# A feed-forward bias taken from a TensorE product and given to VectorE, in a macaron block

## The reference, cut to what matters

```
x = x + 0.5 * ffn(layernorm(x))                 # x: 8 x 512 x 128, float32
x = x + attn(layernorm(x))                      # 16 heads
x = x + 0.5 * ffn(layernorm(x))                 # the same weights again

def ffn(x):                                     # 3 blocks
    h = x
    for blk in range(3):
        i0, i1 = 2 * blk, 2 * blk + 1
        y = qlora_linear(h, ..., biases[i0], ...)      # 128 -> 128
        y = layernorm(y) * ln_gamma[blk] + ln_beta[blk]
        y = gelu(y)
        y = qlora_linear(y, ..., biases[i1], ...)
        h = y + h
    return h
```

## Time and profile before

| | us |
|---|---|
| median of 3 runs | 1030.14 |
| lowest and highest run | 1028.14, 1032.29 |
| the profiled execution's own time | 1026.52 |
| its span, first to last instruction | 1024.7 |
| mean granted TensorE clock | 0.979 of full |

### The profile page before, as it was taken

One profiled execution on the slowest core, in us unless ns is written; L12 is line 12 of the kernel. 1 busy time (PEld: TensorE's weight loads), 2 busy tenths in 40 slices (PEclk: granted clock), 3 DMA queues, 4 the chain that ended last, 5 costly groups with the idle time before them and its releaser, 6 DMA issues.

```text
span 1024.7 us, 22051 instructions
## 1 busy us (share of the span) xinstructions
PE 963.4 (94%) x5892; PEld 502.3 (49%) x5892; DVE 877.1 (86%) x1786; ACT 802.6 (78%) x1293; POOL 784.4 (77%) x706
## 2 busy tenths in 40 slices
PE   4895689999999999999999999999999999997897
PEld 4763234444444444444444444444444444444775
DVE  7667898988888889898888888888888888898566
ACT  4885388888888888888888888888888888886874
POOL 2644168888888888888888888888888888886442
PEclk9999699999999999999999999999999999998999
DMA  9000222222222222222222222222222222220002
GB/s 244 1 2 0 51 50 55 62 61 62 63 63 64 64 65 63 64 64 63 63 64 65 63 64 61 61 61 61 61 61 61 61 61 61 61 62 1 1 1 83
DMA packets 71676, 59.03 MB, mean 58 GB/s; under 512 B 11168, under 2 KB 70560, under 8 KB 71648
## 3 DMA queue, kind: packets, MB, share of 16 engines
q1 hardware_dynamic: 71392, 58.31, 24.0%
q10 hardware_dynamic: 256, 0.39, 0.1%
HBM read 6.23 MB, written 2.10 MB: 8 GB/s over the span
## 4 chain that ended last, share of the span: by engine, by line
PE 83%; DVE 10%; ACT 3%; POOL 2%; issue 1%; DMA 1%; SPq 0%; DVEq 0%; POOLq 0%; ACTq 0%
PE ps L1032 11%; PE ps L1034 10%; PE ps L1033 10%; PE ps L1022 10%; PE ps L1023 10%; PE ps L1015 6%; PE ps L1007 3%; PE ps L953 3%; PE ps L1048 3%; PE ps L1044 3%; PE ps L1045 3%; PE ps L1009 3%; PE ps L1008 3%; PE ps L925 2%; DVE stats L654 1%
## 5 line engine op out<-in xcount | busy, mean ns | idle before, releaser
L376 POOL TENSOR_TENSOR p_lo<-work_b,p_hi 128x1024 f16<-128x1024 f32 x256 | 539.8, 2130 | 129.4 <-ACT p_hi L527 129.3
L794 DVE TENSOR_REDUCE mcol<-ps 128x2 f16<-128x1024 f32 x256 | 301.0, 1220 | 0.8 <-PE ps L1015 0.7
L522 ACT ACTIVATE work_b<-ps,exp_scale 128x1024 f32<-128x1024 f32 x256 | 271.6, 1111 | 32.4 <-PE ps L1023 32.3
L527 ACT ACTIVATE p_hi<-work_b 128x1024 f16<-128x1024 f32 x256 | 256.0, 1054 | 0.0
L1022 PE MATMUL ps<-head_ops 128*128 128x512 f16 x512 | 195.1, 381 | 4.1 <-DVE mcol L794 2.0
L1032 PE MATMUL ps<-p_hi,xn_hi 128*128 128x512 f16 x512 | 195.2, 381 | 0.0
L1023 PE MATMUL ps<-head_ops 128*128 128x512 f16 x512 | 195.1, 381 | 0.0
L1033 PE MATMUL ps<-p_hi,xn_lo 128*128 128x512 f16 x512 | 194.4, 380 | 0.0
L1034 PE MATMUL ps<-p_lo,xn_hi 128*128 128x512 f16 x512 | 194.3, 379 | 0.0
L382 POOL TENSOR_TENSOR x<-x,o_sb 128x512 f32 (+1 forms) x128 | 162.7, 1271 | 8.7 <-DVE o_sb L819 8.7
L804 DVE STREAM_TRANSPOSE head_ops<-mcol 32x128 f16<-32x128 f16 x512 | 155.5, 304 | 9.3
(11 more groups left out here) (116 smaller groups left out, 1316.9 us busy)
## 6 DMA issues: line engine op xcount, KB each, us to landing
head_ops<-pair_ops SPq DMA_DIRECT2D x512, 64.0 KB, 2.0
head_ops<-pair_ops SPq DMA_DIRECT2D x128, 128.0 KB, 2.4
x<-x_dram SPq DMA_DIRECT2D x8, 256.0 KB, 5.9
out<-x SPq DMA_DIRECT2D x8, 256.0 KB, 3.0
vo_last<-wvo_dram SPq DMA_DIRECT2D x1, 1024.0 KB, 13.5
qk<-wq_dram SPq DMA_DIRECT2D x1, 512.0 KB, 5.6
qk<-wk_dram SPq DMA_DIRECT2D x1, 512.0 KB, 6.4
scl<-scales_dram ACTq DMA_DIRECT2D x8, 48.0 KB, 5.2
```

The costliest lines, as they stand in the source:

```text
L376: pool.tensor_tensor(p_lo[:, par, rows, :], p32[:, par, rows, :], p_hi[:, par, rows, :], ALU.subtract).then_inc(plo_done, 1)
L522: nc.scalar.activation(p32[:, par, 2 * a:2 * a + 2, :], s_ps[a], ACT.Exp, scale=exp_scale[:, 0:1]).then_inc(exp_done, 1)
L527: nc.scalar.activation(p_hi[:, par, 2 * a:2 * a + 2, :], p32[:, par, 2 * a:2 * a + 2, :], ACT.Copy).then_inc(phi_done, 1)
L794: nc.vector.tensor_reduce(mcol[:, par, :, t, 0], s_ps[t % 2], AX.X, ALU.max, negate=True).then_inc(max_red, 1)
```

## The change

The bias product of `lin1` and everything that prepared it is gone. The kernel gets the biases once more, as rows in DRAM (`brow_d`); ScalarE's queue loads the three rows of the first linears, spread to all 128 partitions, into `bias_rows` (now float32). VectorE takes the mean of each row and subtracts it (five instructions). A new `add_bias(f, i)` on VectorE adds the row to `bank[b]` and writes `work_b`, once for each batch of a unit. `squares` then reads `work_b` and writes its squares (which nothing reads) to the bank, and `z_scaled` multiplies `work_b` in place. The additions of units 0 and 1 stand ahead of the norm's means (for f = 0 between and behind the statistics); those of units 2 and 3 stand in rounds 1 and 2 in front of the seed; those of units 4 to 11 at the end of rounds 3 to 10. `weight_maxima(0)` and `(1)` move to rounds 0 and 1, in front of `z_scaled`.

```diff
+            act.dma_start(bias_rows[:, :, :], brow_d[0:NL:2, :].partition_broadcast(128)).then_inc(bias_in, 16)
...
                 for c, b in unit_batches(i):
-                    act.wait_ge(lin1_done, at(f, i, c))
+                    act.wait_ge(zb_ready, at(f, i, c))
...
-                        ins = nc.scalar.activation(work_b[:, b, cols], bank[b][:, cols], ACT.Square,
+                        ins = nc.scalar.activation(bank[b][:, cols], work_b[:, b, cols], ACT.Square,
...
-            link(dve, nc.vector.tensor_tensor(bias_c[:, :], bias[:, 0:NL:2], ps[:, SG + 2, 0:NL:2], ALU.subtract))
-            link(dve, nc.vector.tensor_tensor(bias_mid[:, :], bias_c[:, :], bf16_top(bias_c), ALU.subtract))
-            nc.vector.tensor_copy(bias_parts[:, :, 0], bf16_top(bias_c))
-            nc.vector.tensor_copy(bias_parts[:, :, 1], bf16_top(bias_mid))
-            nc.vector.tensor_tensor(bias_parts[:, :, 2], bias_mid[:, :], bf16_top(bias_mid),
-                                    ALU.subtract).then_inc(bias_split, 1)
...
+            dve.wait_ge(bias_in, 16)
+            link(dve, nc.vector.tensor_reduce(row_mean[:, :], bias_rows[:, :, :], AX.X, ALU.add))
+            link(dve, nc.vector.tensor_scalar(row_mean[:, :], row_mean[:, :], -1.0 / D, None, ALU.mult))
+            for n in range(NB):
+                ins = nc.vector.tensor_scalar(bias_rows[:, n, :], bias_rows[:, n, :], row_mean[:, n:n + 1], None,
+                                              ALU.add)
+            link(dve, ins)
+
+            def add_bias(f, i):
+                n = i // UNITS
+                row = bias_rows[:, n, :].rearrange("p (a d) -> p a d", a=1).to_broadcast([128, TT, D])
+                for c, b in unit_batches(i):
+                    dve.wait_ge(lin1_done, at(f, i, c))
+                    nc.vector.tensor_tensor(work_b[:, b, :].rearrange("p (t d) -> p t d", d=D),
+                                            bank[b].rearrange("p (t d) -> p t d", d=D), row,
+                                            ALU.add).then_inc(zb_ready, 1)
...
-                    nc.vector.tensor_tensor(work_b[:, b, :].rearrange(tiles, d=D), bank[b].rearrange(tiles, d=D),
-                                            scale.to_broadcast([128, TT, D]), ALU.mult).then_inc(z_full, 1)
+                    zb = work_b[:, b, :].rearrange(tiles, d=D)
+                    nc.vector.tensor_tensor(zb, zb, scale.to_broadcast([128, TT, D]), ALU.mult).then_inc(z_full, 1)
...
                 if f:
+                    add_bias(f, 0)
                     norm_stats([B - 1])
+                    add_bias(f, 1)
                 else:
-                    norm_stats(range(SG, B), loaded=True)
+                    norm_stats(range(SG, SG + 2), loaded=True)
+                    add_bias(f, 0)
+                    norm_stats(range(SG + 2, B), loaded=True)
+                    add_bias(f, 1)
                 norm_means(1)
...
+                    if i in (1, 2):
+                        add_bias(f, i + 1)
                     if i < STEPS:
                         seed(f, i)
+                    if f == 0 and i in (0, 1):
+                        weight_maxima(i)
                     if 1 <= i <= STEPS:
                         z_scaled(f, i - 1)
-                    if f == 0 and i in (2, 3):
-                        weight_maxima(i - 2)
+                    if 3 <= i < STEPS - 1:
+                        add_bias(f, i + 1)
...
-                    nc.tensor.matmul(bank[b].rearrange("p (t d) -> p t d", d=D), ones_b[:, :], row,
-                                     start=True, stop=False)
                     for t in range(TT):
                         ins = nc.tensor.matmul(bank[b][:, t * D:(t + 1) * D], hT[:, b, t * 128:(t + 1) * 128],
-                                               wt[:, 2 * n, :], start=False, stop=(t == TT - 1))
+                                               wt[:, 2 * n, :], start=True, stop=True)
```

More of the change, by code:

```diff
@@ L19, with macaron @@
 AX = mybir.AxisListType
-def macaron(nc, x_d, q_d, k_d, vo_d, qw_d, sc_d, bias_d, la_d, lb_d, gam_d, bet_d, out_d):
+def macaron(nc, x_d, q_d, k_d, vo_d, qw_d, sc_d, bias_d, la_d, lb_d, gam_d, bet_d, brow_d, out_d):
     B, T, D = x_d.shape
@@ L56, in macaron @@
         ident = sb("ident", [128, 128])
-        ident_b = sb("ident_b", [128, 128], BF16)
         mean_mat = sb("mean_mat", [128, 128])
@@ L101, in macaron @@
         u_u = sb("u_u", [128, 2 * TT])
[L102 to L105, removed]
+        bias_rows = sb("bias_rows", [128, NB, D])
+        row_mean = sb("row_mean", [128, NB])
         hT = sb("hT", [128, B, T])
@@ L147, in macaron @@
         prep_pe = sem("prep_pe")
[L148 to L151, removed]
+        bias_in = sem("bias_in")
+        zb_ready = sem("zb_ready")
         prep_v = sem("prep_v")
@@ L311, in _ @@
             pool.memset(mean_mat[:, :], 1.0 / D).then_inc(consts, 1)
-            pool.memset(ones_b[:, :], 1.0)
-            pool.memset(bias_rows[:, :, :], 0.0).then_inc(bias_clear, 1)
             pool.wait_ge(prep_p, 1)
@@ L357, in _ @@
                     fold_last(4 * i + 2)
-            pool.wait_ge(prep_a, 3)
+            pool.wait_ge(prep_a, 2)
             pool.tensor_tensor(w_lo[:, :, :], qk32[:, :, :], w_hi[:, :, :], ALU.subtract).then_inc(prep_p, 1)
-            pool.wait_ge(prep_a, 5)
+            pool.wait_ge(prep_a, 4)
             pool.tensor_tensor(vo_lo[:, :, :], vo32[:, :, :], vo_hi[:, :, 0:D], ALU.subtract).then_inc(prep_p, 1)
@@ L416, in _ @@
                 act.dma_start(scl[16 * s:16 * s + 16, :, :], sc_d[s].partition_broadcast(16)).then_inc(sc_in, 16)
-            act.wait_ge(consts, 2)
-            nc.scalar.activation(ident_b[:, :], ident[:, :], ACT.Copy).then_inc(prep_a, 1)
+            act.dma_start(bias_rows[:, :, :], brow_d[0:NL:2, :].partition_broadcast(128)).then_inc(bias_in, 16)
             def pre(f, s):
@@ L462, in weight_halves @@
                 if i == 10:
-                    act.wait_ge(prep_a, 2)
+                    act.wait_ge(prep_a, 1)
                     for n in range(2):
@@ L486, in ffn @@
                 pre(f, 0)
[L487 to L491, removed]
                 for i in range(STEPS + 3):
@@ L886, in _ @@
             pe.wait_ge(consts, 2)
-            nc.tensor.matmul(ps[:, SG + 2, 0:NL], mean_mat[:, :], bias[:, :], start=True, stop=True)
             for n in range(NL):
@@ L904, in pre @@
                     turn(bank[b], lambda t: xhat[:, b * TT + t, :], pre_t)
-            def turn_bias():
-                pe.wait_ge(bias_split, 1)
-                pe.wait_ge(prep_a, 1)
-                for n in range(NB):
-                    ins = nc.tensor.matmul(ps[0:3, SG + 3, n * D:(n + 1) * D], bias_parts[:, n, :], ident_b[:, :],
-                                           start=True, stop=True)
-                ins.then_inc(bias_turned, 1)
             def lin1(f, i):
@@ L920, in lin1 @@
                         pe.wait_ge(h_ready, (f * NB + n - 1) * B + b + 1)
-                    row = bias_rows[:, n, :].rearrange("p (a d) -> p a d", a=1).to_broadcast([128, TT, D])
-                    nc.tensor.matmul(bank[b].rearrange("p (t d) -> p t d", d=D), ones_b[:, :], row,
-                                     start=True, stop=False)
                     for t in range(TT):
                         ins = nc.tensor.matmul(bank[b][:, t * D:(t + 1) * D], hT[:, b, t * 128:(t + 1) * 128],
-                                               wt[:, 2 * n, :], start=False, stop=(t == TT - 1))
+                                               wt[:, 2 * n, :], start=True, stop=True)
                     ins.then_inc(lin1_done, 1)
@@ L967, in ffn @@
                     pre(0, 0)
-                    turn_bias()
                     pe.wait_ge(prep_v, 1)
-                    pe.wait_ge(bias_ready, 1)
                 for i in range(STEPS + 3):
@@ L995, in _ @@
             ffn(0)
-            pe.wait_ge(prep_a, 5)
+            pe.wait_ge(prep_a, 4)
             pe.wait_ge(prep_p, 10)
@@ L1148 @@
         "ln_beta": a["L0_ffn_ln_beta"].T,
+        "bias_rows": a["L0_ffn_biases"],
     }
```

3 lines of the change are left out of this document (removed).

## The result

| | before | after |
|---|---|---|
| median of 4 runs each, us | 1029.14 | 1053.95 |
| lowest to highest, us | 1027.93 to 1032.29 | 1053.64 to 1054.76 |
| profiled execution, us | 1026.52 | 1053.9 |
| its span, us | 1024.7 | 1052.0 |

The ratio is 1.0232 with an interval of 1.0206 to 1.0258: the change costs 24.8 us. The prediction had the direction (+12.9 us) and half the size, and 1053.95 lies outside its range of 1035 to 1051.

The account below looks back on a forecast made before the run. TensorE was taken to bound the steady steps, with VectorE's and GpSimd's queues holding the heads. Second feed-forward +2.8, first +6.6, operand places +2, clock +1.5: +12.9 on 1030.14, so 1043.0 us, range 1035 to 1051.

Parts of the forecast that it names:

- Read and write places: Both feed-forwards: z with two SBUF operands and GpSimd's Newton pieces hold each other up; +2 us, bounds 0 to +7.
- port: The prediction's word for z with two SBUF operands and GpSimd's Newton holding each other up; +2 us taken.
- Squares from SBUF into PSUM: ScalarE's squares, eight per step: ±0.03 us each, so ±2 us in the second feed-forward, ±1 in the first; taken as nothing.
- First feed-forward, head: Start of the first feed-forward: work added on VectorE delays seeds and z; +5.9 us where TensorE resumes, +6.6 to its end.
- Second feed-forward, head: Start of the second feed-forward: additions before the norm delay transposes 2.6 us and unit 4's product about 3.4 us.
- faster rival: Additions ahead of the norm fall into VectorE's waits, heads cost nothing, TensorE's savings remain: −4.7, 1025 us; chance 0.04.
- what stands in front of the norm is paid in full: Heads of both feed-forwards: work put on VectorE before the norm delays the chain by its full length; four additions, 2.6 us.
- The steady step: Second feed-forward's steady steps: VectorE and ScalarE in turn set 4.54 us, not 4.81; −1.9 us over seven steps.
- TensorE would show as no longer full: Sign in the profile after: steady steps near 4.55 to 4.7 us, TensorE no longer full, VectorE above 90%.
- TensorE's clock: TensorE's clock falls at a new place; +1.5 us, bounds 0 and 2.
- Hidden: ScalarE's new load and the removed bias preparation cost or gain nothing; without cover, each below 0.5 us.

Follow-up runs that it names:

- e1: Changed kernel, with GpSimd's two long subtractions started only after z of unit 11 of the first feed-forward; 1047.33 us, ratio 1.0172.
- e2: Changed kernel, with the bias added in place in PSUM, where squares and z read it; 1039.24 us, ratio 1.0104 to the kernel before.
- e9: Changed kernel, with the squares' unused output written to SBUF instead of PSUM, still reading SBUF; 1051.94 us, ratio 1.0217.
- e12: Changed kernel with the sum left in PSUM and no additions for units 0 to 3 (that computation left out); 1030.62 us, ratio 0.9995.
- e10: Changed kernel, with additions of units 0 and 1 behind the second half's norm and ScalarE's order fitted to it; 1054.52 us, ratio 1.0240.
- e8: Changed kernel, with 30 unused transposes on TensorE before its wait for weight_maxima(2) in the first feed-forward; 1049.76 us, ratio 1.0181.
- e7: Kernel before, with additions in place in PSUM for units 4 to 11 of the second feed-forward, seed between the two z; 1028.03 us, ratio 0.9974.
- e6: Kernel before, with additions in place in PSUM replacing the bias product for units 4 to 11 of the second feed-forward only; 1027.29 us, ratio 0.9960.

## Why the prediction was right in direction and short in size

**The account.** Of the 24.8 us, 6.6 are z 11 beside the long subtractions (after minus e1). 8.1 are the rest of what e2 gained (e1 minus e2): some 6 for the operands' places, and some 2 for TensorE's lower clock in the head, which is in the profiles of after and e1 and not in those of e2 and e9. 9.7 are left in e2, and the additions of the first four units account for all of them (e12). Together 24.4.

**The step that failed: "Read and write places".** It had the right instructions and the right mechanism, and was mis-sized: +2, with bounds of 0 and +7, where e2 shows 14.7 together with the squares, or some 12.7 without the head's clock. Two things were left out. The bound was built from z against Newton's pieces of 0.2 us; but GpSimd's queue also holds two subtractions of 4 us, and the trace of before had both facts (`w_lo` from 85.82 to 89.90, z 11 at 87.46 in 1.28 us). Each z of unit 11 waited for the end of the subtraction that was running, so the longest neighbour sets the bound, and 6.6 us lay there. Secondly, in the GpSimd-paced head each z holds up a Newton (a piece of 0.65 us at 51.57, 0.20 otherwise) and is itself held up by a fold (2.33 us for the pair at 49.83), and the z come one after another on the chain: 2.6 us from z 1 to z 4 (after against e2). The rows at 101.01 to 110.01 show the waiting, 7.90 us against e1's 1.28. What in the chip makes the two wait, for which the prediction has the name port, no run shows.

**"Squares from SBUF into PSUM" taken as nothing.** That was the second miss. The eight pairs take 2.46 us instead of 2.19, 0.03 each (0.27 over eight, 34 ns), the size and sign that the earlier trace rows had shown for a read; they were rounded away. Over seven steps it is 1.9 us, about two thirds of the 2.9 by which e2's second feed-forward beats after's (71.8 against 74.7); three of the squares on the first's chain add 0.8. The place of the result made no difference: the eight pairs take 2.46 us with either destination (after, e9).

**"First feed-forward, head" and "Second feed-forward, head": right in mechanism, and the close sum is in part luck.** Seed 0 was put at 32.1 and came at 32.33. With operands in PSUM, TensorE resumed 6.8 us later (e2), where 5.9 was predicted. e2's whole of +9.7 stands against 9.4 for the two feed-forwards and 1.5 for the clock, but the parts are not as predicted. In e2's profile the first feed-forward is 9.9 us longer than in that of before (6.6 predicted; the terms given for it add to 6.4), the second 1.1 (2.8 predicted), and the attention 1.6. Of the 9.9, 2.9 are two `lin2` at a lower clock: 3.18 us instead of 1.72 behind the gap (0.66 over 61 to 66), 3.38 instead of 1.98 at `lin2(9)` (0.61 over 93 to 97). The faster rival fails: the heads cost 9 to 11 us, far above the 4.7 from which it decides. That what stands in front of the norm is paid in full did not hold: with the additions behind the norm (e10) the shift comes 2.8 us earlier and z 0 only 0.3. z 0 comes 7.2 us later than before (39.74, not 32.50), where 5.7 was predicted and e9, at the higher clock, has 6.4. The path is the predicted one: seed 0 is 3.6 later, and behind it stand the maxima, the additions of unit 2 with their wait for TensorE, and seed 1.

**"The steady step": right in mechanism.** VectorE and ScalarE in turn set it. Predicted 4.54; 4.69 with the slower squares, 4.42 without (e2). VectorE's share came to 86% (19.82 of 23), not above 90. That TensorE would show as no longer full was wrong as a sign: the view counts it busy for 23.00 of 23.

**"TensorE's clock": right that it falls at a new place, too small, and one place missed.** No run shows the +1.5 as such. What the runs showed in its place: the wait ahead of `lin2` was 4.37 us, 2.54 before, and the granted clock over 66 to 75 was 0.75, where e8, with the wait filled, has 1.00. The bound of 2 came from the one low stretch of before, 0.81 over 958 to 966 behind a wait of 3.70 us. The head was not thought of: over 40 to 44 the granted clock is 0.59 in after and 1.00 in before, and by e9 that is 1.9 us. e8 gave back 4.2 by medians (after's four runs lie within 1.1 us, e8's within 0.5), 3.3 of them before the attention. That the old gap leaves the clock at 1.00 over 52 to 61 held for the profiled executions of before and e7, not for e6's (0.81). The 4.2 of e8 is no further term: it lies inside what the account above gives to the first four units and to the operands.

**"Hidden": right** as far as the chain shows: neither the load nor the removed preparation stands on it.

## What to carry to other kernels

When an edit leaves a product of VectorE with both inputs in SBUF, as z here, list everything that GpSimd has in its queue beside each use, and price the waiting by the longest of them, not by the typical one: here by the 4.07 and 4.36 us of the two subtractions, not by Newton's 0.2. Work taken from the engine that bounds the average may land in a stretch that another engine bounds: here the same addition cost 9 to 11 us over the first four units and brought 4.0 us where it was made only for the last eight units of the second feed-forward. Price each stretch by itself, and make the move only where the receiving engine waits. And before two profiles are compared, compare their granted clocks stretch by stretch: 1.9 us of what looked like the operands' price in the head was the clock's, and one more version with the same instructions (e9) told them apart.

## What the runs showed of the hardware

- A product of VectorE with both inputs in SBUF stood still behind GpSimd subtractions of 4.07 and 4.36 us: 7.90 us for two, against 1.28 with one input in PSUM beside the same subtraction (before, e2) or with the subtractions held back (e1).
- ScalarE's squares over 128 elements with an accumulator cost 0.03 us more each from SBUF than from PSUM (eight in 2.46 us, not 2.19; after, e2), and the same whether they write to PSUM or to SBUF (2.46; after, e9).
- An addition of 128x512 in place in PSUM took VectorE 0.62 us (e2), one from PSUM to SBUF 0.61 (after).
- With transposes without use in a wait of 4.4 us (e8) TensorE's granted clock stayed at 1.00 over the 9 us behind it (0.75 without them), and the kernel was 4.2 us faster, of which 3.0 can be placed behind the gap in the first feed-forward.
- The same instructions ran at different granted clocks from one execution to another: 1.00 and 0.59 over 40 to 44 (e9, after), 1.00 and 0.81 over 52 to 61 (e7, e6), with 1.9 and 2.0 us between them.
